# Pre-norm graph layer in fp16 pairs: L's block sums and the normalised x held in PSUM, row ends and splits on the vector engine, GpSimd left with small vectors

## The reference, cut to what matters

```python
h = relu(layernorm(x))                    # x: 8 x 2048 x 128, float32
HW = einsum('bnf,fo->bno', h, W)          # W: 128 x 128
A = relu((adj + adj.T) * 0.5)             # adj: 2048 x 2048
D = sum(A, axis=1); d = D ** -0.5
L = eye(2048) - d[:, None] * A * d[None, :]
out = x + relu(einsum('nm,bmo->bno', L, HW))
```

## Time and profile before

| what | us |
|---|---|
| median of 3 runs | 437.81 (436.41, 437.81, 440.29) |
| the profiled execution | 435.52 |
| its span, first to last instruction | 433.7 |
| around the span | 1.8 |
| PE busy | 379.2 (87%) |
| DVE busy | 309.9 (71%) |
| ACT busy | 178.1 (41%) |
| POOL busy | 185.0 (43%) |
| mean granted TensorE clock | 0.968 of full |

### The profile page before, as it was taken

How to read it: one execution, slowest core, us unless ns; L and a number is a source line. 1 busy time by engine, 2 the same in 40 slices (tenths; PEclk the granted TensorE clock), 3 DMA queues, 4 the chain that set the end, 5 groups by cost and what they waited for, 6 DMA issues and landing times.

```text
span 433.7 us, 6127 instructions
## 1 busy us (share of the span) xinstructions
PE 379.2 (87%) x2097; PEld 198.4 (46%) x2097; DVE 309.9 (71%) x696; ACT 178.1 (41%) x379; POOL 185.0 (43%) x247
## 2 busy tenths in 40 slices
PE   3528778987799999997999994999999999999993
PEld 3528753433244444434454542544444444444441
DVE  2787999978579999899887685138845972885142
ACT  1555977554267678758844112102301320132010
POOL 0197702078976566475520551241415252432102
PEclk9877999999999999998999997999999999999998
DMA  8999994101244414332434027940131023103203
GB/s 272 354 371 385 383 273 125 26 0 59 65 121 131 124 39 130 104 97 82 149 119 147 0 73 249 348 143 13 49 97 51 0 74 90 30 26 97 74 0 97
DMA packets 72990, 54.98 MB, mean 127 GB/s; under 512 B 3200, under 2 KB 64768, under 8 KB 72960
## 3 DMA queue, kind: packets, MB, share of 16 engines
q1 hardware_dynamic: 72960, 54.60, 39.9%
HBM read 39.91 MB, written 14.68 MB: 126 GB/s over the span
## 4 chain that ended last, share of the span: by engine, by line
DVE 25%; issue 24%; POOL 17%; DMA 14%; PE 9%; SPq 5%; ACT 5%; POOLq 0%; DVEq 0%; ACTq 0%
DMA out_dram<-sums 7%; POOL form L540 5%; DMA sums<-in_x_dram 4%; POOL hbuf L497 4%; POOL sums L519 4%; DVE form L823 3%; DVE S L768 3%; SPq L363 3%; DMA S<-in_adj_dram 2%; DVE stats L728 2%; PE ps L1087 2%; PE ps L1088 2%; PE ps L1089 2%; DVE S L749 2%; DVE form L815 1%
## 5 line engine op out<-in xcount | busy, mean ns | idle before, releaser
L1087 PE MATMUL ps<-S,hbuf 128*128 128x512 f16 x240 | 91.5, 381 | 6.9 <-DVE S L768 6.9
L1088 PE MATMUL ps<-S,hbuf 128*128 128x512 f16 x256 | 97.5, 381 | 0.0
L519 POOL TENSOR_TENSOR sums<-res,sums 128x512 f32<-128x512 f32 x32 | 46.8, 1462 | 117.1 <-DVE res L885 106.3
L1089 PE MATMUL ps<-S,hbuf 128*128 128x512 f16 x240 | 91.2, 380 | 0.0
L1099 PE MATMUL ps<-S,hbuf 128*128 128x512 f16 x160 | 61.3, 383 | 0.0
L1100 PE MATMUL ps<-S,hbuf 128*128 128x512 f16 x160 | 61.2, 382 | 0.0
L1101 PE MATMUL ps<-S,hbuf 128*128 128x512 f16 x160 | 61.1, 382 | 0.0
L540 POOL TENSOR_TENSOR form<-hbuf 128x1024 f32<-128x1024 f16 x16 | 35.1, 2205 | 31.8 <-DVE S L835 16.9
L664 ACT ACTIVATE g<-ps 128x512 f16<-128x512 f32 x32 | 18.5, 589 | 72.7 <-DVE ps L860 24.4
L621 ACT ACTIVATE S<-S,dneg 128x512 f16<-128x512 f32 x54 | 37.7, 714 | 18.9 <-DVE S L768 17.0
L1037 PE MATMUL ps<-ident,S 128*128 128x128 f32 x160 | 24.4, 318 | 20.1 <-issue 12.0
(11 more groups left out here) (117 smaller groups left out, 688.1 us busy)
## 6 DMA issues: line engine op xcount, KB each, us to landing
S<-in_adj_dram SPq DMA_DIRECT2D x16, 1024.0 KB, 12.1
hbuf<-in_x_dram SPq DMA_DIRECT2D x64, 128.0 KB, 3.4
sums<-in_x_dram SPq DMA_DIRECT2D x32, 256.0 KB, 2.8
out_dram<-sums SPq DMA_DIRECT2D x32, 256.0 KB, 2.3
t_forms<-form SPq DMA_DIRECT2D x48, 128.0 KB, 1.8
S<-t_forms SPq DMA_DIRECT2D x5, 1024.0 KB, 9.5
S<-t_forms SPq DMA_DIRECT2D x1, 768.0 KB, 10.7
S<-t_forms SPq DMA_DIRECT2D x1, 256.0 KB, 8.8
```

Source lines behind the costliest of these rows:

```text
L519: nc.gpsimd.tensor_tensor(sums[:, e % SUMS, :], res[:, e % 2, :], sums[:, e % SUMS, :], ALU.add).then_inc(sum_ready, 1)
L1087: nc.tensor.matmul(acc, h_hi, l_hi(t), start=(mt == 0), stop=False)
L1088: nc.tensor.matmul(acc, h_hi, l_lo(t), start=False, stop=False)
L1089: last = nc.tensor.matmul(acc, h_lo, l_hi(t), start=False, stop=(mt == T - 1))
```

## The change

GpSimd keeps only the vectors of 8 values of the layer norm, the normalising of units 0 to 7, and the row scales. `add_x`, `join_pair` and its `split_h_lo` are gone from it, and so is the normalising of units 8 to 15.

- Row ends: `take_product` becomes `finish_product` on DVE, two instructions (scale in PSUM in place; relu and add of x into sums); res is not used for it. There are three sums buffers, not two. W and finish move: `W_AT` (7, 10), `TAKE_AT` (9, 12), in the parts `w_at` and `taken_in`.
- Units 8 to 31: ACT normalises into PSUM bank 5, DVE splits the lo for all. The slots of units 8 to 15 move.
- Forms: each is made in PSUM bank 4, one at a time, by `form_t`; ACT rounds it into work, DVE subtracts from PSUM, and one DMA in place of two spills hi and lo together. The fourth piece of a round (T3) is split later, two in each of parts 0 to 3; the diagonal pieces of rows 8 to 15 are taken with the forms.
- So the plain steps have four banks for sums, not six (`PLAIN_ACCS`).
- Pairs: DVE adds hi and lo itself into one pair buffer. Two pairs of the first quarter are combined before part 0 (slots 114 and 119, four before), the other two in parts 0 and 1; later quarters likewise two and two.

```diff
-W_AT = (5, 7)
-ADD_AT = (8, 10)
-STORE_AT = (11, 13)
+W_AT = (7, 10)
+TAKE_AT = (9, 12)
+STORE_AT = (11, 14)
+FIRST_W_AT = (3, 6)
+FORM_AT = (1, 3, 5)
 FORM_HI = (2, 4, 6)
 FORM_LO = (3, 5, 7)
 FORM_OUT = (5, 7, 9)
-CHAIN_HI = (4, 5, 6, 7)
-CHAIN_LO = (5, 6, 7, 8)
-PAIR_AT = (4, 5, 6)
+CHAIN_HI = (3, 4, 5)
+CHAIN_LO = (4, 5, 6)
+PAIR_AT = (4, 5)
 SUM_AT = (2, 5, 6)
-W_PART_AT = ((3, 1), (6, 0), (6, 7))
+W_PART_AT = ((4, 3), (6, 3), (7, 4), (8, 4))
 ACCS = 6
-XN = 1
-SUMS = 2
+SUMS = 3
 FORM_SLOTS = 4
+PLAIN_ACCS = 4
...
-    h_slot += [16, 18, 20, 22, 24, 26, 28, 30]
+    h_slot += [13, 15, 18, 20, 23, 25, 28, 31]
...
-    first_pair_slot = [T * (PLAIN - 1) + 3 * p for p in range(UNITS // 2)]
+    first_pair_slot = [T * (PLAIN - 1) + 2, T * (PLAIN - 1) + 7]
...
-        p1_v = S[:, HALF - 1:T:HALF, 7 * WIDE // 2:4 * WIDE]
...
-        def pair_buf(n):
-            return form[:, n % 2 * 2:n % 2 * 2 + 2, :]
+        p1_v, w_u = (work[:, i, :] for i in (2, 3))
+        pair_buf = work[:, 0:2, :]
...
+        T_BANK, XN_BANK = 4, 5
...
-            return x_buf(u, b0, b1) if u < 2 * UNITS else xn[:, u % XN, b0 * P:b1 * P]
+            return x_buf(u, b0, b1) if u < UNITS else ps[:, XN_BANK, b0 * P:b1 * P]
...
-            i, r = (t - STEPS) // 4, (t - STEPS) % 4
-            return [(i, 2), (i + HALF, 2), (i + HALF, 3), (i, 3)][r]
+            if t >= T3_FROM:
+                return t - T3_FROM, 3
+            i, r = (t - STEPS) // 3, (t - STEPS) % 3
+            return [(i, 2), (i + HALF, 2), (i + HALF, 3)][r]
...
-                return e % ACCS
+                return e % PLAIN_ACCS
...
-            if k in PAIR_AT and q + 1 < QUARTERS:
-                return (q + 1) * (UNITS // 2) + PAIR_AT.index(k)
-            return q * (UNITS // 2) + UNITS // 2 - 1 if q and k == 0 else None
+            if k < 2:
+                return q * (UNITS // 2) + 2 + k
+            return (q + 1) * (UNITS // 2) + PAIR_AT.index(k) if k in PAIR_AT and q + 1 < QUARTERS else None
+        def w_at(r, i):
...
+            if r == 0 and i in FIRST_W_AT:
+                return [PLAIN_TILES - 2 + FIRST_W_AT.index(i)]
+            if r == PARTS - 1 and i == HALF - 1:
+                return [TILES - 2]
+            tiles = [PLAIN_TILES + 4 * q + W_PART_AT.index((k, i))] if (k, i) in W_PART_AT else []
+            if q and (k + len(ORDER), i) in W_PART_AT:
+                tiles.append(PLAIN_TILES + 4 * (q - 1) + W_PART_AT.index((k + len(ORDER), i)))
+            return tiles
         def taken_in(r):
...
             e = PLAIN_TILES + 4 * q
-            if k < 2:
-                return [e - 2 + k] if q else []
-            return {3: [e], 6: [e + 1]}.get(k, [])
+            if r == 1:
+                return [e - 2, e - 1]
+            if r == PARTS - 1:
+                return [e + 1]
+            return [e] if k == 5 else [e - 3 + k] if q and k < 3 else []
...
-                sp.dma_start(t_forms[n % 3, 0, n // 3], form16[:, (n - 1) % FORM_SLOTS, WIDE:2 * WIDE]).then_inc(t_out[n % 3], 16)
-                sp.dma_start(t_forms[n % 3, 1, n // 3], form16[:, n % FORM_SLOTS, 0:WIDE]).then_inc(t_out[n % 3], 16)
+                sp.dma_start(t_forms[n % 3, n // 3], form16[:, n % FORM_SLOTS, :]).then_inc(t_out[n % FORM_SLOTS], 16)
...
-            def split_h_lo(u):
...
-            def add_x(e):
-                pool.wait_ge(prod_taken, e + 1)
-                pool.wait_ge(sums_in[e % SUMS], 16 * (e // SUMS + 1))
-                nc.gpsimd.tensor_tensor(sums[:, e % SUMS, :], res[:, e % 2, :], sums[:, e % SUMS, :],
-                                        ALU.add).then_inc(sum_ready, 1)
...
-            def join_pair(n):
-                q, p = n // (UNITS // 2), n % (UNITS // 2)
-                u = q * UNITS + 2 * p
-                pool.wait_ge(h_lo_ready, 2 * UNITS)
-                pool.wait_ge(h_lo2_ready, 2 * UNITS)
-                if n < 2:
-                    for f in range(3):
-                        pool.wait_ge(t_out[f], 32 * HALF)
-                if n >= 2:
-                    pool.wait_ge(s_lo_ready, n - 1)
-                nc.gpsimd.tensor_tensor(pair_buf(n), hbuf[:, u:u + 2, 0, :], hbuf[:, u:u + 2, 1, :], ALU.add).then_inc(pair_ready, 1)
...
-                act.wait_ge(rstd_ready, k - 2 * UNITS // LN_BATCH + 1)
-                if u >= 2 * UNITS + XN:
-                    act.wait_ge(h_lo2_ready, u - XN + 1 - 2 * UNITS)
+                act.wait_ge(rstd_ready, k - UNITS // LN_BATCH + 1)
+                if u > UNITS:
+                    act.wait_ge(h_lo_ready, u)
...
-                act.wait_ge([t1_ready, t2_ready, t4_ready][n % 3], n // 3 + 1)
-                if n % 3 == 1:
-                    act.wait_ge(t4_ready, n // 3 + 1)
-                if n:
-                    act.wait_ge(t_lo_ready, n)
-                nc.scalar.activation(form16[:, (n - 1) % FORM_SLOTS, WIDE:2 * WIDE], form[:, n % FORM_SLOTS, :],
-                                     ACT.Copy).then_inc(t_hi_ready, 1)
+                act.wait_ge(t_ready, n + 1)
+                if n >= FORM_SLOTS:
+                    act.wait_ge(t_out[n % FORM_SLOTS], 16 * (n // FORM_SLOTS))
+                nc.scalar.activation(form16[:, n % FORM_SLOTS, 0:WIDE], ps[:, T_BANK, :], ACT.Copy).then_inc(t_hi_ready, 1)
...
-            def second_form(i):
-                n, mt = 3 * i + 1, i + HALF
-                dve.wait_ge(t1_ready, i + 1)
-                if i:
-                    dve.wait_ge(t_out[0], 32 * i)
-                    dve.wait_ge(t_out[1], 32 * i)
-                nc.vector.scalar_tensor_tensor(form[:, n % FORM_SLOTS, :], s_piece(chain_of("B22", i)), dneg[:, mt:mt + 1],
-                                               form[:, (n - 1) % FORM_SLOTS, :], ALU.mult, ALU.subtract).then_inc(t2_ready, 1)
...
+            def form_t(n):
+                i, f = n // 3, n % 3
+                t = ps[:, T_BANK, :]
+                if n:
+                    dve.wait_ge(t_lo_ready, n)
+                if f == 0:
+                    dve.wait_ge(b12_ready, i + 1)
+                    nc.vector.scalar_tensor_tensor(t, s_piece(chain_of("B11", i)), npos[:, i:i + 1],
+                                                   s_piece(chain_of("T3", i)), ALU.mult, ALU.add).then_inc(t_ready, 1)
+                else:
+                    mt = i + HALF
+                    nc.vector.scalar_tensor_tensor(t, s_piece(chain_of(["B22", "B21"][f - 1], i)), dneg[:, mt:mt + 1], t,
+                                                   ALU.mult, ALU.subtract).then_inc(t_ready, 1)
...
             def combine_pair(n):
-                dve.wait_ge(pair_ready, n + 1)
-                a11, a21, a12, a22 = (pair_buf(n)[:, :, i * P:(i + 1) * P] for i in range(4))
+                q, p = n // (UNITS // 2), n % (UNITS // 2)
+                u = q * UNITS + 2 * p
+                dve.wait_ge(h_lo_ready, UNITS * QUARTERS)
+                if n:
+                    dve.wait_ge(s_lo_ready, n)
+                else:
+                    wait_spilled(dve)
+                nc.vector.tensor_tensor(pair_buf, hbuf[:, u:u + 2, 0, :], hbuf[:, u:u + 2, 1, :], ALU.add).then_inc(s_chain, 1)
+                a11, a21, a12, a22 = (pair_buf[:, :, i * P:(i + 1) * P] for i in range(4))
...
-            def take_product(e):
+            def finish_product(e):
...
-                if e >= 2:
-                    dve.wait_ge(sum_ready, e - 1)
-                nc.vector.scalar_tensor_tensor(res[:, e % 2, :], ps[:, 6 + e % 2, :], 0.0, dsv[:, slot, :],
-                                               ALU.max, ALU.mult).then_inc(prod_taken, 1)
+                dve.wait_ge(sum_ready, e)
+                dve.wait_ge(sums_in[e % SUMS], 16 * (e // SUMS + 1))
+                prod = ps[:, 6 + e % 2, :]
+                nc.vector.tensor_tensor(prod, prod, dsv[:, slot, :], ALU.mult).then_inc(prod_scaled, 1)
+                dve.wait_ge(prod_scaled, e + 1)
+                nc.vector.scalar_tensor_tensor(sums[:, e % SUMS, :], prod, 0.0, sums[:, e % SUMS, :], ALU.max,
+                                               ALU.add).then_inc(sum_ready, 1)
...
-                    if u < 2 * UNITS:
-                        split_h_lo(u)
-                if tau < T - LEAD - 1:
+                    split_h_lo(u)
+                if tau < HALF - LEAD - 1:
                     take_diag(tau + LEAD + 1)
...
-                    if form_slot[i] + 2 == tau:
-                        if i == 0:
-                            dve.wait_ge(d_ready, 3)
-                        first_form(i)
-                        third_form(i)
-                        second_form(i)
-                        fourth_form(i)
                     for f in range(3):
                         if form_slot[i] + FORM_LO[f] == tau:
                             split_t_lo(3 * i + f)
-                    for r in range(4):
+                    for f in range(3):
+                        if form_slot[i] + FORM_AT[f] == tau:
+                            if i == 0 and f == 0:
```

(25 more changed lines are left out.)

195 lines of the change are left out of this document (77 added, 118 removed).

## The result

The changed kernel takes 413.49 us in the median (411.73, 412.28, 414.69, 415.0) against 437.88 for the kernel before, measured beside it: 0.944 of it, with a 95% interval of 0.937 to 0.950. That is 24.4 us less; 21.8 were forecast. A few executions in these experiments ran at a clearly lower clock; they stand in the medians given, while the ratios leave them out.

What follows compares the result with a forecast made beforehand. PE bounds the kernel and only its gaps, 26.8 us waiting or at lower clock, can be won; gains 7.5 + 3.6 + 7.8 + 2.7 + 0.2 = 21.8 off 437.8 give 416.0 us, 8 in 10 range 410 to 430.

Steps and rivals of the forecast that it cites:

- Step 1: Step 1: GpSimd's 16 us of normalising leave the chain; loss about 0.5 us instead of 8.0, gain 7.5.
- E: Rival: gaps stay, lo of h merely changes engine, ACT as late as POOL was; 433 us or more, chance 0.05.
- Steps 2 to 5: Steps 2 to 5: DVE 13.6 us late at slot 80; PE loses 3.8 in place of 7.4, gain 3.6.
- cover of 9.8: Plain steps: DVE lateness, 9.8 us, that the later products by W absorb before PE waits; 7.2 before.
- queue of 69.0: Slots 32 to 80: DVE's summed work without waits, 69.0 us, 2.8 over the 66.2 PE needs.
- B: Rival: DVE still bounds the plain steps; a quarter of 40 bank handovers cost 1.22 us each, 425 us, chance 0.18.
- C: Rival: every one of 40 handovers in slots 33 to 112 costs 1.22 us; slower, 449 us, chance 0.05.
- Part 0: Part 0: g of tiles 14 and 15 comes in time; loss 0.5 us in place of 8.3, gain 7.8.
- Four pairs stand ahead of g: Part 0 before the change: four pairs precede g on DVE, begun after POOL waited 10.58 us for the last spill.
- Quarters and end: Later quarters: DVE's slack suffices, gain 2.7 of 3.1 us; last tile: gain 0.2.
- Prices: Assumed instruction costs: DVE 0.58 with PSUM input, 0.67 to 0.79 for SBUF forms, pair sum 1.3; ACT 2.22 a unit.
- the sign that was asked for: Sign of being right, in the changed profile: the clock is 1.00 from step 0 to the end.

Runs made afterwards that it cites:

- pool_norm: The changed kernel, but GpSimd normalises units 8 to 15 again, in place in hbuf, slots otherwise as changed: 419.58 us, 0.954 of the kernel before.
- changed_again: The changed kernel as it is, run once more in the third group beside the kernel before: 413.38 us, 0.941 of the kernel before.
- idle adds: The changed kernel with 30 additions on GpSimd, reading SBUF, that nothing waits for, forms still in PSUM: 421.19 us, 0.958 of the kernel before.
- four_pairs: The changed kernel, but all four pairs of the first quarter are combined before part 0, none in parts 0 and 1: 414.66 us, 0.942 of the kernel before.
- before_dve_pairs: The kernel before, but DVE sums hi and lo of all 16 pairs; GpSimd still adds x: 434.96 us, 0.989 of the kernel before.

## Why the prediction was right, and where it was off

The forecast of 416.0 stands 2.5 us above the result, inside its own range, and its sign and size hold. Step 1 was right in its mechanism; in steps 2 to 5 two errors of opposite sign partly cancelled, and in part 0 the number was near for a cause that was only half the one given. That much was luck. By its steps:

- **Step 1**, gain 7.5: the stretch gave 7.5, with 0.4 lost as forecast (0.5). pool_norm takes the cause away from the slots and gives it to GpSimd's normalising. E, the rival by which ACT would be as late, is out.
- **Steps 2 to 5**, gain 3.6: 4.9 were won. The lateness at step 2 was priced at 6.8 and was 7.0; at step 5 at 13.6 and was 12.1; with a cover of 9.8 the loss is 2.5 in place of 3.8. The two terms inside were each off: from 110.49 to 176.67 DVE is idle for 66.18 - 38.93 - 20.63 = 6.6 us where I took 4 for its waits, so that its queue of 69.0 was overpriced by some 4. B and C, the chain of the forms through one bank, are out: the idle time ahead of its forms' lo is 0.0 in the sum of 24 (the last column of L769 above), and 0.6 for the 16 later forms. But the other bank, of the units, has such waits: 5.8 of the 6.6 us are DVE's for ACT's hi of a unit (L714, above). So B, which counted the units' 16 handovers with the forms' 24, named a wait that is real, but only for the units and at half its price of 12. W's later slots, which the forecast named for their cover, carry 6.2 us of the result.
- **Part 0**, gain 7.8: 8.2 were won, for a reason that I weighted wrongly. "Four pairs stand ahead of g" was the picture; with four pairs still ahead, the changed kernel loses only 1.5 there. What part 0 had lost was above all GpSimd's share: its first sum ahead of DVE, and its sums and adds of x beside combinations, which read two operands from SBUF. DVE's way from the first pair to g falls from 28.0 us to 26.4 when only the sums leave GpSimd, and to 23.4 when the adds of x are gone as well, with four pairs in all three. Moving only the sums in the kernel before brings 4.5 of the 8.2 in that stretch, more than half of it by the clock.
- **Quarters and end**, gain 2.9: 1.3 + 0.6 + 0.6 + 0.6 = 3.1. The slack was there: DVE is busy for 28.87 of 38.94 us in the second quarter, where the forecast counted 34 and left the slowing by GpSimd in it. The lo of pair 3 costs part 2 0.69 in the changed kernel, where part 2 was counted as just in time.
- **Prices.** DVE's sum of a pair was 1.26 for the 1.3 taken; the 0.065 us more for a source in PSUM that the forecast worked out from the Trainium skill ("VectorE: DVE Perf Modes", section on the TRN2 errata), and did not follow, isn't there: the same subtraction takes 675 ns from PSUM and 679 from SBUF. The forecast read the 1.75 us of DVE beside GpSimd as what the two engines cost each other whenever they work at once; that instruction (L800) reads S and form, both in SBUF, and this is what it takes.
- **What I did not see**: that one part of the change was a loss. The 4.3 us that row ends add to DVE up to step 5 stand in the sum, but nothing set them against leaving the add on GpSimd. That costs the changed kernel 4.5 us. And the clock: 1.00 from step 0 to the last tiles, the sign that was asked for, is what the first profile shows; in changed_again step 5 has 0.94.

The parts do not add up: W later, with row ends and stores, is worth 6.2 us in the changed kernel and minus 3 in the one before, since there the last spill and the pairs come no earlier and the next reloads later. The idle adds cost 7.8 us because they meet a DVE queue near its bound.

## What to carry to other kernels

Before winning slack in an early stage, follow the chain that the next stage waits for (here a spill behind a store on SP's queue, the pairs behind the spill, the reloads behind both): if this chain does not start earlier, the slack is paid back there. Between GpSimd and VectorE it was here less their load that counted than which instructions of VectorE read two operands from SBUF; those with one of them in PSUM ran beside GpSimd's additions at their usual time. So when an engine is freed, look for the instruction that can go back to it without being waited for, and try each part of a large change with that part alone undone.

## What the runs showed of the hardware

The same gap can cost the clock or not. In step 5 of the changed kernel PE waits 2.34 us in one profiled execution and 2.35 in the other (changed_again). Busy time by stretch behind the gap, in the first:

```profile
189.00:192.00 3.00, 2.47 (x21) 1.53 (x22) 2.96 (x7) 2.56 (x7) 0.67 (x3) 1.00 0.23 87
192.00:196.00 4.00, 4.00 (x29) 2.16 (x28) 3.47 (x6) 2.92 (x7) 1.54 (x4) 1.00 0.05 17
```

and in the second:

```profile
189.00:192.00 3.00, 2.28 (x18) 1.32 (x19) 2.96 (x8) 2.56 (x8) 0.58 (x4) 0.83 0.23 87
192.00:196.00 4.00, 4.00 (x15) 1.59 (x14) 3.47 (x6) 2.92 (x8) 1.73 (x4) 0.70 0.00 0
```

Fifteen matmuls in place of twenty-nine: after the gap TensorE stood part of the time at the lower of its levels, 1.2 GHz (granted 0.83 and then 0.70 of full), and the step took 26.26 us for 24.57. That is 1.7 of the 1.9 us between these two executions. Step 5 of four_pairs took 26.27 with the same gap; the other executions of the changed kernel were not traced, and how often it happens stays open, as does why. The length of a gap alone does not tell: the 3.54 us at part 0 of before_dve_pairs left the clock at 1.00 in its row above.
